# Quartered GpSimd additions, earlier query/key pieces and stack transfers, and an output rotation put into the next layer

## The reference, cut to what matters

```python
x = _L0_cond_ref(x, ...)                       # stencils on 512x512 fields
# transformer layer, 16 heads of 32
q, k, v = x@Wq+bq, x@Wk+bk, x@Wv+bv
scores = where(mask, -inf, q@k.T/sqrt(32) + attention_bias)
x = x + (softmax(scores) @ v) @ Wo + bo
x = x + gelu2((_ln(x)*g2+beta2) @ W1 + b1) @ W2 + b2
# adapter
h = gelu(x @ down_W.T + down_b); h = expert(h) + domain_emb
x = _ln(h @ up_W.T + up_b + x) * ln_gamma + ln_beta
# rotation of column pairs
out = [x0*ct + x1*st, -x0*st + x1*ct, x2*cp + x3*sp, -x2*sp + x3*cp]
```

## Time and profile before

| | us |
|---|---|
| median of 3 runs | 4777.39 (4770.36 to 4782.34) |
| span of the profiled execution | 4771.2 |
| one layer (from one layer's end to the next) | about 267 |
| PE busy | 4186.0 |
| DVE, ACT, POOL busy | 2611.2, 2466.4, 1289.7 |

### The profile page before, as it was taken

How to read it: one execution, slowest core, us unless ns; L and a number is a source line. 1 busy time by engine, 2 the same in 40 slices (tenths; PEclk the granted TensorE clock), 3 DMA queues, 4 the chain that set the end, 5 groups by cost and what they waited for, 6 DMA issues and landing times.

```text
span 4771.2 us, 70346 instructions
## 1 busy us (share of the span) xinstructions
PE 4186.0 (88%) x25480; PEld 3020.1 (63%) x25720; DVE 2611.2 (55%) x5784; ACT 2466.4 (52%) x4664; POOL 1289.7 (27%) x653
## 2 busy tenths in 40 slices
PE   6994898989889888988889898988889898988887
PEld 3442676766667676766667676766667676766665
DVE  8993546364554546364554546364555536464553
ACT  0001746456473746456473746456473746556472
POOL 0001141423223141423323141423324141423313
PEclk9996999999999999999999999999999999999998
DMA  3224636455363636445363636455363636445361
GB/s 123 107 98 139 186 126 200 135 151 166 110 194 107 186 126 199 135 144 173 110 189 111 186 126 200 135 147 165 106 195 113 182 130 183 145 129 183 98 185 45
DMA packets 530310, 700.10 MB, mean 147 GB/s; under 512 B 45216, under 2 KB 250832, under 8 KB 529968
## 3 DMA queue, kind: packets, MB, share of 16 engines
q1 hardware_dynamic: 512560, 660.98, 45.4%
q10 hardware_dynamic: 16896, 33.56, 1.8%
q0 software_dynamic: 512, 1.05, 0.1%
HBM read 527.20 MB, written 33.62 MB: 118 GB/s over the span
## 4 chain that ended last, share of the span: by engine, by line
PE 56%; DVE 11%; SPq 7%; ACT 6%; issue 5%; DMA 3%; POOL 3%; another core or an unknown queue 0%; POOLq 0%; DVEq 0%; ACTq 0%
PE bank L840 34%; SPq L535 6%; PE bank L921 5%; PE bank L885 5%; PE bank L909 4%; PE bank L944 4%; PE bank L910 2%; DVE prob L1099 2%; DMA stack<-parts 2%; DVE parts L1174 2%; DMA V<-in_L_cond_W 1%; ACT probT L713 1%; ACT prob L692 1%; DVE parts L1084 1%; PE bank L849 1%
## 5 line engine op out<-in xcount | busy, mean ns | idle before, releaser
L619 POOL TENSOR_TENSOR w<-w_raw,w 128x1024 fp32r<-128x1024 f32 x240 | 580.6, 2419 | 2033.8 <-ACT w L683 1902.3
L692 ACT ACTIVATE prob<-prob,low 128x512 f32<-128x512 f32 x1024 | 736.7, 719 | 166.0 <-DVE low L1099 166.0
L1174 DVE TENSOR_TENSOR parts<-gel,parts 128x512 fp32r<-128x512 f32 x256 | 261.5, 1021 | 893.6 <-ACT parts L808 893.6
L713 ACT ACTIVATE probT<-bank 128x512 f32<-128x512 f32 x1024 | 608.3, 594 | 244.3 <-PE bank L921 229.5
L921 PE MATMUL bank<-ident,prob 128*128 128x128 f32 x4096 | 638.7, 280 | 96.4 <-ACT probT L713 67.9
L1099 DVE CUSTOM_DVE_ANT_0 prob<-bank,prob 128x512 f32<-128x512 f32 x1024 | 696.8, 681 | 0.0
L921 PEld LDWEIGHTS bank<-ident,prob 128*128 128x128 f32 x4096 | 500.9, 144 | 204.3 <-issue 77.2
L909 PE MATMUL bank<-stack 128*128 128x512 f32 x1024 | 485.2, 476 | 101.1 <-DMA stack<-parts 54.5
L1098 DVE COPY fence<-cur 128x1 f32<-128x1 f32 x1024 | 155.7, 152 | 664.4 <-PE bank L910 325.7
L619 POOL TENSOR_TENSOR stack<-V,stack 128x1024 fp32r<-128x1024 f32 x144 | 352.0, 2446 | 597.3 <-ACT stack L683 593.4
L840 PE MATMUL bank<-xT,stack 128*128 128x512 f32 x1920 | 490.1, 404 | 24.9 <-DVE xT L1070 13.9
(11 more groups left out here) (174 smaller groups left out, 5809.9 us busy)
## 6 DMA issues: line engine op xcount, KB each, us to landing
prob<-in_fside_Bx16xSxS SPq DMA_DIRECT2D x512, 512.0 KB, 4.9
stack<-parts SPq DMA_DIRECT2D x1024, 128.0 KB, 2.4
V<-in_L_cond_W SPq DMA_DIRECT2D x256, 256.0 KB, 3.6
w_raw<-in_L_cond_W SPq DMA_DIRECT2D x256, 256.0 KB, 2.9
field<-in_x SPq DMA_DIRECT2D x16, 1024.0 KB, 5.4
x<-total ACTq DMA_DIRECT2D x16, 1024.0 KB, 5.9
xin<-x SPq DMA_DIRECT2D x16, 1024.0 KB, 5.6
w_raw<-in_L_cond_Wv SPq DMA_DIRECT2D x64, 256.0 KB, 2.8
```

What stands on the lines that cost most here:

```text
L619: pool.tensor_tensor(w[s][:, 1, :], w_raw[s], w[s][:, 0, :].bitcast(F32), ALU.subtract).then_inc(w_lo[s], 1)
L692: act.activation(prob[:, i, :], prob[:, i, :], ACT.Exp, bias=low[:, i:i + 1], scale=-1.0, accum_out=total[:, g % 2, i:i + 1]).then_inc(exp ...
L713: act.activation(probT[:, i % 8, :], turned[e % 2][:], ACT.Copy).then_inc(turned_copied[e % 2], 1)
L1174: v.tensor_tensor(parts[:, 2 * (f % 2) + 1, :], gel[:, f % 2, :], parts[:, 2 * (f % 2), :].bitcast(F32), ALU.subtract).then_inc(g_lo, 1)
```

## The change

The three GpSimd row additions become four instructions each, one per row block (`add_row`). In groups 0 and 1 the pieces of group g+2's product are issued in steps 3 to 13, its drains are moved from the next group into steps 11, 12, 14 and 15 of group g, and its 16 stack transfers stand in SP's queue at p = 7 of group g, ahead of the last bias pair of group g+1. The transfers for group 1 stay where they were. Ahead of group 0, group 1's pieces come three at a time after score blocks 3 to 6. Gamma and beta go to GpSimd, as eight instructions behind its last `split_lo` of the layer; the rotation goes to VectorE's steps 0 to 5 of group 1 of the next layer; the store goes to SP, in group 2. The fence copies read another tile.

```diff
+QK_FIRST, QK_SPAN, QK_EVICT = 3, 11, (11, 14)
 # SP
+                def group_stacks(b, g):
+                    sp.wait_ge(qk_hi, 8 * b + 2 * g + 2)
+                    sp.wait_ge(qk_lo, 8 * b + 2 * g + 2)
+                    for j in range(HG):
+                        load_stack(b, g, j)
+                def store_out(b):
+                    sp.wait_ge(out_ready, b + 1 + START)
+                    sp.dma_start(rows_of(out, b), res[:]).then_inc(out_done, 16)
                 def group(b, g):
                     for p in range(8):
-                        if p == 2:
-                            sp.wait_ge(qk_hi, 2 * n + 4)
-                            sp.wait_ge(qk_lo, 2 * n + 4)
-                            for j in range(HG):
-                                load_stack(b, g + 1, j)
+                        if p == 2 and g == 0:
+                            group_stacks(b, 1)
+                        if p == 3 and g == 2 and b:
+                            store_out(b - 1)
...
                         sp.wait_ge(probT_full, ENTRIES * b + entry(g, 2 * p + 1) + 1 + START)
+                        if p == 7 and g + 2 < G:
+                            group_stacks(b, g + 2)
                         load_bias(b, g + 1, p // 2, p % 2)
 # GpSimd
+                def add_row(dst, src, name, signal):
+                    for q in range(TB):
+                        ins = pool.tensor_tensor(dst[:, q, :], src[:, q, :], row[name][:], ALU.add)
+                    ins.then_inc(signal, 1)
-                    pool.tensor_tensor(xin[:], xin[:], bcast(row["bo"]), ALU.add).then_inc(xin_biased, 1)
+                    add_row(xin, xin, "bo", xin_biased)
-                    pool.tensor_tensor(res[:], res[:], bcast(row["b2"]), ALU.add).then_inc(res_biased, 1)
+                    add_row(res, res, "b2", res_biased)
-                    pool.tensor_tensor(res[:], tok[:], bcast(row["up_b"]), ALU.add).then_inc(y_biased, 1)
+                    add_row(res, tok, "up_b", y_biased)
                         split_lo(0, ITEMS[0] * (b + 1) + W0_QK + 1)
+                    pool.wait_ge(normed, b + 1)
+                    for q in range(TB):
+                        pool.tensor_tensor(res[:, q, :], res[:, q, :], row["gamma"][:], ALU.mult).then_inc(gained, 1)
+                    pool.wait_ge(gained, TB * (b + 1))
+                    for q in range(TB):
+                        ins = pool.tensor_tensor(res[:, q, :], res[:, q, :], row["beta"][:], ALU.add)
+                    ins.then_inc(shifted, 1)
 # ScalarE
-                        if i in (0, 1) and not last:
-                            q_hi(b, g + 1, i, FILL_QK + g + 1)
+                        if first and i in (0, 1):
+                            q_hi(b, 1, i, FILL_QK + 1)
+                        if g + 2 < G and i in QK_EVICT:
+                            q_hi(b, g + 2, QK_EVICT.index(i), FILL_QK + g + 2)
-                    act.wait_ge(out_ready, b + 1 + START)
-                    act.dma_start(rows_of(out, b), res[:]).then_inc(out_done, 16)
 # TensorE
-                        if g + 2 < G and i >= 5:
-                            for p in range((i - 5) * 12 // 11, (i - 4) * 12 // 11):
+                        if g + 2 < G and 0 <= i - QK_FIRST < QK_SPAN:
+                            for p in range((i - QK_FIRST) * QK_PIECES // QK_SPAN, (i - QK_FIRST + 1) * QK_PIECES // QK_SPAN):
                                 qk_piece(b, g + 2, p)
-                        if i:
-                            for p in range(2):
-                                qk_piece(b, 1, 2 * (i - 1) + p)
+                        if i >= 3:
+                            for p in range(3):
+                                qk_piece(b, 1, 3 * (i - 3) + p)
 # VectorE: drains as on ScalarE, in steps 11, 12, 14, 15; fence from minus_half instead of cur
+                        if g == 1 and i < len(TAIL):
+                            if b:
+                                turn_out(b - 1, i)
+                        if g == 1 and i == len(TAIL):
+                            v.wait_ge(out_ready, b + START)
+                            link(v.tensor_copy(cur[:], scal[:, b:b + 1, :].rearrange("p o c -> p (o c)")))
-                    link(v.tensor_tensor(res[:], res[:], bcast(row["gamma"]), ALU.mult))
-                    link(v.tensor_tensor(res[:], res[:], bcast(row["beta"]), ALU.add))
-                    # the two scalings and four combinations of the rotation: now turn_out(b, step)
```

More of the change, by code:

```diff
@@ L440, in layers @@
         y_ready, y_biased, hid_wide, hid_ready, mixed, out_ready = (sem(n) for n in ("y_ready", "y_biased", "hid_wide", "hid_ready", "mixed", "out_ready"))
+        normed, gained, shifted = (sem(n) for n in ("normed", "gained", "shifted"))
         rows_of = lambda t, b: t[b:b + 1].rearrange("o (t p) c -> p (o t) c", p=P)
@@ L579, in _ @@
                     load_rows(sp, 1, ITEMS[1] * b + W1_O, Wo, 2)
[L581 to L584, removed]
+                    group_stacks(b, 0)
                     load_qk(sp, 0, ITEMS[0] * b + W0_QK + 2, 2)
@@ L609, in _ @@
                         load_second_qk(sp, b + 1)
+                store_out(B - 1)
             @block.gpsimd
@@ L1097, in score_step @@
                         v.wait_ge(bias_in[i // HG][i % HG // 2], 16 * (4 * b + g + 1))
-                    v.tensor_copy(fence[:, i % 7:i % 7 + 1], cur[:, 0:1])
+                    v.tensor_copy(fence[:, i % 7:i % 7 + 1], minus_half[:, 0:1])
                     v.tensor_tensor_reduce(prob[:, i, :], score[i % 2][:], prob[:, i, :], -1.0, MIN_START, ALU.add, ALU.min,
@@ L1122, in group @@
                             invert(b, g)
[L1123 to L1126, removed]
+                        if first and i in (0, 1):
+                            qk_wide(b, 1, i, FILL_QK + 1)
+                        if first and i in (2, 3):
+                            qk_lo_part(b, 1, i - 2)
+                        if g + 2 < G and i in QK_EVICT:
+                            qk_wide(b, g + 2, QK_EVICT.index(i), FILL_QK + g + 2)
+                        if g + 2 < G and i - 1 in QK_EVICT:
+                            qk_lo_part(b, g + 2, QK_EVICT.index(i - 1))
+                        if g == 1 and i == 0:
+                            if b:
+                                v.wait_ge(shifted, b)
+                        if g == 1 and i < len(TAIL):
+                            if b:
+                                turn_out(b - 1, i)
+                        if g == 1 and i == len(TAIL):
+                            v.wait_ge(out_ready, b + START)
+                            link(v.tensor_copy(cur[:], scal[:, b:b + 1, :].rearrange("p o c -> p (o c)")))
                         if (g, i - 1) in CTX_PARTS:
@@ L1134, in first_qk, with turn_out @@
                         qk_lo_part(b, 0, c)
+                TAIL = range(6)
+                quads = res[:].rearrange("p t (q c) -> p (t q) c", c=4)
+                sines = tok[:].rearrange("p t (q c) -> p (t q) c", c=4)
+                def turn_out(b, step):
+                    if step < 2:
+                        h = step
+                        link.mark(v.tensor_scalar(sines[:, :, 2 * h:2 * h + 2], quads[:, :, 2 * h:2 * h + 2], cur[:, 4 + 2 * h:5 + 2 * h], None, ALU.mult))
+                        return
+                    if step == 2:
+                        link.sync()
+                    a = step - 2
+                    h, c = divmod(a, 2)
+                    o = 2 * h + 1 - c
+                    ins = v.scalar_tensor_tensor(quads[:, :, a], quads[:, :, a], cur[:, 3 + 2 * h:4 + 2 * h], sines[:, :, o],
+                                                 ALU.mult, ALU.add if c == 0 else ALU.subtract)
+                    if a < 3:
+                        link.mark(ins)
+                    else:
+                        ins.then_inc(out_ready, 1)
+                        link.sync()
                 link = Link(v, dve_step)
@@ L1142, in _ @@
                 first_qk(0)
-                assert link.n == FIRST_STEPS, link.n
+                v.wait_ge(half_set, 1)
+                link(v.tensor_copy(cur[:], scal[:, 0:1, :].rearrange("p o c -> p (o c)")))
                 for b in range(0, B):
-                    link = Link(v, dve_step, STEPS * b + FIRST_STEPS)
-                    v.wait_ge(out_ready, b + START)
-                    link(v.tensor_copy(cur[:], scal[:, b:b + 1, :].rearrange("p o c -> p (o c)")))
                     for i in range(S_LEAD):
@@ L1221, in _ @@
                     for q in range(TB):
[L1222 to L1241 removed]
+                        ins = normalise(res, res, q)
+                    ins.then_inc(normed, 1)
+                v.wait_ge(shifted, B)
+                for step in range(len(TAIL)):
+                    turn_out(B - 1, step)
 def program(nc, x, dt, step_id, bias, domain, theta, phi, mask, A_grid, B_grid, W_ada, b_ada, Wq, bq, Wk, bk, Wv, bv,
```

19 lines of the change are left out of this document (removed).

## The result

The changed kernel takes 4836.9 us (median of 4 runs, 4834.9 to 4839.9) against 4779.0 (4770.4 to 4782.3): a ratio of 1.0125, 95% interval 1.0111 to 1.0140. I had forecast 4757 and a range up to 4820; it is slower, and beyond the range. The profiled execution has a span of 4833.0 us against 4771.2, 61.8 more.

The account below looks back on a forecast made before the run. TensorE sets the time, 27 us a layer to be had. -5.0 + 2.5 + 1.2 - 0.4 = -1.7 us a layer, 15 times, first layer -1, end +6: 4757 us from 4779.0; range 4680 to 4820.

Parts of the forecast that it names:

- signs of being right: Step 3's piece awaits the split; low part below 2.5 us; block 14 awaits bias in groups 1, 2; no group 3 stack wait.
- The wait of step 3's piece: In group 0, TensorE's first piece for group 2 waits 2.7 us for weights behind GpSimd's split.
- a sign of being wrong: No such bias wait, a quarter far from 1.33 us, or VectorE still locked over several quarters.
- Boundary: At the layer boundary, with the rotation gone, score blocks 0 to 3 precede the split; group 0 starts 3.1 us earlier.
- Group 0, the step that failed first: In group 0 the lock on VectorE's low parts goes; with the boundary -5.0 us a layer, between -7.4 and -2.5.
- the rival of GpSimd's longer queue: GpSimd's queue holds the first group: only -2.5 there, net +0.8 us a layer, 4795 us; chance 0.16.
- Group 1: Up to step 9: +3.0 for the late bias, less 1.0 for earlier pieces, 0.5 for the clock: +2.5 us a layer.
- Group 2, the mis-sized term: Up to step 11: +1.4 for the late bias, -0.2 for fewer ScalarE conversions: +1.2 us a layer.
- Late bias as a rival: In groups 1 and 2 the last bias pair lands after 4.9 us: 3.6 more a layer, 4812 us; chance 0.19.
- Rotation in group 1: VectorE's added work in group 1 costs nothing; up to 1 us if the bias came in time.
- Feed-forward and end: Quarters of b2 free VectorE, -0.4 us a layer; gamma and beta unhidden after the last layer, +6.0 once.

Follow-up runs that it names:

- the swap: The changed kernel with the last bias pair issued ahead of the 16 stack transfers in SP's queue, not behind them; 4729.3 us, ratio 0.989.
- y3_rotation_only: The kernel x3_late_qk with bo, b2 and up_b each added whole, in one instruction instead of quarters; 4833.7 us, ratio 1.0114.
- x3_late_qk: The changed kernel with the pieces, drains and stack transfers of groups 2 and 3 put back as before; 4822.1 us, ratio 1.0083.
- v2_no_rotation: The kernel before with quarters, earlier pieces, drains and stack transfers, and last bias pair first; rotation, gamma, beta, store as before; 4673.1 us, ratio 0.9780.

## Why the prediction was wrong

The sum was -1.7 us a layer, and +3.8 were measured. Of the 5.5 us between them the boundary with group 0 has 3.0, group 2 has 2.1 and group 1 has 0.6. Of the signs of being right, the waits for the bias in groups 1 and 2 came, and the wait for the stack of the last group went. The wait of step 3's piece did not come, the low part was not below 2.5 us, and a sign of being wrong came: VectorE locked over several quarters. Step by step:

- **Boundary.** Forecast 3.1 us, measured 2.3 (15.12 to 12.84). Right in kind: the split is no longer awaited (0.29 us). The stack's transfers, now the later, hold TensorE 1.12 us instead, which I had not named.
- **Group 0, the step that failed first.** "VectorE's two low parts are done before GpSimd comes to bo, and the lock on them goes." With the boundary this was to give -5.0, at worst -2.5; measured -2.28 + 0.29 = -2.0 (12.84 - 15.12 and 31.73 - 31.44). Two things were off. I looked only at bo and not at the split before it. And I had the split start 5.2 us after the group (1017.7 against 1012.5), behind the first low part; it started 2.5 us after it. TensorE's lead took longer: the 24 piece matmuls took 8.2 us and not 5.9, with a granted clock of 0.64 from 1008.2 to 1013.0. And GpSimd's queue was quicker: the eight additions took 10.1 us from 1008.1 to 1018.2, not 10.6, and the gather 1.02 us, not 1.7. So the low part came into the split. From there my reading of the earlier trace rows, "VectorE gets in at a boundary of GpSimd instructions", does not hold: of 14 low parts that came into the split in the changed kernel, or 0.1 us ahead of it, none got in at any of four boundaries; of 16 that came into the first quarter in the quarters alone, all got in at the next. The third step's wait for the weights, 2.7 us, did not come; the rival of GpSimd's longer queue was right about the place (gamma, beta and the gather push the split into VectorE's way). Its -2.5 had the second low part wait for the 2.39 us of the split; it was the first that waited, and for the four quarters too.
- **Group 1.** Forecast +2.5, measured +3.1. Stack issues from 1.34 us after the group's start (forecast 1.3) for 11.74 us (10.7), landing 3.8 (3.7). The chain was right. The row of 10.66 that I took was a quick one: the 16 issues take 10.2 to 11.8 us before and after alike, on the mean of the inner layers 11.1 before and 11.3 here.
- **Group 2, the mis-sized term.** Forecast +1.2, measured +3.3. The mechanism was right: VectorE waits 4.70 us for the pair, TensorE 4.49. The size was not, by five pieces (means over the inner layers). Step 9 starts at 17.3 and not 16.4: the issues take 11.1 us, the landing 3.95 and the way from it to TensorE 0.9, where I had 10.7, 3.7 and 0.7: +0.9. Steps 9 and 10 take 5.3 us, not "two steps with a product with V, 2.9": +2.4, of which the slow clock that falls into them is 1.7 (3.80 us at 0.55) and the rest stays open. From step 11 on the group is quicker, 6.8 us against 9.0, as the slow clock is over: -2.2. And step 11 of before stood at 17.9 in the layer that I took as the pattern, and at 17.1 on the mean: +0.8. The 0.2 credited for ScalarE's conversions is the fifth; no run shows it by itself.
- **Late bias as a rival.** It was to cost 3.6 more a layer and give 4812. Groups 1 and 2 cost 2.7 more than my sum, at its place, though not by its landing of 4.9 us (3.8 in the rows), and the swap gave 108 us. The total of 4837 lies beyond it because of group 0. I gave it 0.19; its "for" (strict order, a fixed need) rested on rows, its "against" (first of its burst) turned out to be true and beside the point, as 11.7 us of issues lie ahead of it in that layer.
- **Rotation in group 1.** "I cost it at nothing." In the changed kernel the late bias covers most of it. With the bias in time it costs 1.4 us a layer (15.56 against 14.17), 20 us, where I had said up to 1 us. Where the four drains stand in the same steps of VectorE, as in `y3_rotation_only`, the way to step 9 is 4.1 us longer than before (17.51 against 13.44). The row shows one scaling of 2.50 us beside a split of 2.38 in the place of 0.76. This is the first half of the rule from the Trainium skill (GPSIMD Engine Reference, Key points: GpSimd contends with VectorE's two-port modes); I had left it out of the sum. The trace agrees in 15 of 15 layers as far as the wait goes; that the scaling runs in such a mode no row says. Spreading the six instructions removed both this and their density; which part of the 20 us is which was not told apart.
- **Feed-forward and end.** Forecast -0.4 and +6.0. Measured -0.6 a layer. Of the 10.1 in the last layer 5.9 are its lead and groups and 4.2 the part behind them; with the -0.6 that is in it, the end cost 4.8. Quarters cost 1.23 us back to back in gamma and beta (4.92 for four), as forecast between 1.13 and 1.33. The store on SP, put at nothing, cost nothing in the changed kernel (last group 9.83 as before), but see the last group of `x3_late_qk`.

What I judged as one change were three with interactions. The quarters are worth 62 us alone and 3 within the changed kernel, because the rotation part moved the low part's arrival from the quarter into the split: with the earlier pieces and without the rotation (`v2_no_rotation`) it still comes 0.31 to 0.33 us into the first quarter and is let in, in all 16 layers. The earlier pieces cost 15 us as they were made (4822 to 4837), and are worth 43 beside the quarters once the bias pair goes first (4716.5 to 4673.1).

Open: why an arrival in the split is passed over at each boundary and one in a quarter is not. One low part in the changed kernel came 0.24 us into the first quarter and was passed over three times (5.27 us), another 0.32 us into it was let in at the next boundary (1.50), so it is not the kind of GpSimd instruction alone. The instant sorts every case: over the six kernels with quarters and no added wait, the 60 low parts that began at most 0.24 us into the first quarter were passed over, and the 36 that began 0.30 to 0.33 us into it were let in. One wait ended it; the mechanism is not shown.

## What to carry to other kernels

When transfers are moved ahead of others in a queue that is strictly in order, work out the due time of each neighbour, and put the few with a fixed need before the many: one issue ahead of sixteen, twice a layer, was worth 108 us here. When two engines can lock each other out, ask at which instant the victim arrives, not only how long the lock is; whatever moves one engine's queue moves that instant, and a gain measured alone (62 us) can be gone in company. Where GpSimd instructions follow each other without a wait, one wait at the boundary where the other engine stands can free it, at the price of a gap of 0.08 us here.

## What the runs showed of the hardware

- VectorE's low part (512 columns, two SBUF inputs), 0.68 us alone, took 6.33 us beside a split of 2.38 us and four additions of 1.24 that followed without a gap, and 7.49 beside the split and one addition of 4.51. With a gap of 0.08 us after the split it ended 0.56 us after the split did. The Trainium skill (GPSIMD Engine Reference, Key points) says that GpSimd contends with VectorE instructions that have two SBUF inputs. These rows agree, and show one such wait that lasts over five GpSimd instructions.
- A quarter beside which VectorE gets in is itself slower: the four of bo took 5.90 us with two low parts let in, and 4.96 with none.
- A GpSimd addition of 512 columns takes 1.28 us as a median and 1.24 in a row of four, against 4.51 for 2048 in one: four cost 0.45 us more than one.
